# Rows in groups of five instead of four, tiles handled in pairs, and filler matmuls in a mixture-of-experts kernel

## What is computed

```python
t = _to_tokens(x)                                   # (8, 1024, 64)
logits = einsum('bsd,de->bse', _ln_t(t), gate_w) + gate_b
top_probs, top_idx = top_k(softmax(logits), 2)      # 2 of 16 experts
top_probs = top_probs / sum(top_probs)
hidden = silu(einsum(x, w1)) * einsum(x, w2)        # hidden size 128, per expert
out = sum over the 2 chosen experts of prob * einsum(hidden, w3)
x = _from_tokens(t + out)
```

## Time and profile before

| | us |
|---|---|
| median of 3 runs (lowest, highest) | 378.61 (377.3, 378.87) |
| the profiled execution | 376.88 |
| span in its profile, first to last instruction | 374.8 |
| TensorE busy in the span | 298.6 (80%) |
| VectorE | 268.9 (72%) |
| ScalarE | 221.5 (59%) |
| GpSimd | 179.5 (48%) |
| mean granted TensorE clock | 0.762 of 2.4 GHz |

### The profile page before, as it was taken

One profiled execution on the slowest core, in us unless ns is written; L12 is line 12 of the kernel. 1 busy time (PEld: TensorE's weight loads), 2 busy tenths in 40 slices (PEclk: granted clock), 3 DMA queues, 4 the chain that ended last, 5 costly groups with the idle time before them and its releaser, 6 DMA issues.

```text
span 374.8 us, 8710 instructions
## 1 busy us (share of the span) xinstructions
PE 298.6 (80%) x2802; PEld 251.6 (67%) x2802; DVE 268.9 (72%) x716; ACT 221.5 (59%) x484; POOL 179.5 (48%) x157
## 2 busy tenths in 40 slices
PE   4879567957476677469999998998878895799996
PEld 4737346855255554259998987888777784588884
DVE  1964574497999954959999967467878885883762
ACT  4878844562177675449898985455555552555431
POOL 2016263330088785445655650077865400887880
PEclk9959985555855568659999999898999996555555
DMA  7999900000012121242545454455544512233432
GB/s 222 338 260 385 387 24 0 2 2 0 0 45 53 50 56 35 65 118 47 137 117 139 114 133 90 99 138 142 132 106 107 128 37 53 50 103 87 111 79 70
DMA packets 55390, 39.89 MB, mean 106 GB/s; under 512 B 37660, under 2 KB 49692, under 8 KB 54708
## 3 DMA queue, kind: packets, MB, share of 16 engines
q1 hardware_dynamic: 42804, 29.25, 27.5%
q0 software_dynamic: 12384, 10.10, 11.3%
q10 hardware_dynamic: 160, 0.01, 0.0%
HBM read 20.08 MB, written 19.14 MB: 105 GB/s over the span
## 4 chain that ended last, share of the span: by engine, by line
PE 36%; DVE 26%; ACT 11%; issue 10%; DMA 8%; POOL 4%; SPq 2%; DVEq 1%; POOLq 0%; ACTq 0%
PE banks L978 7%; PE banks L872 4%; DMA w_raw<-in_L_ffn_w 4%; POOL xs L1485 4%; PE banks L966 4%; PE banks L965 4%; DVE tok L1292 4%; DMA xs<-sorted_y,back 3%; DVE cand L1378 3%; PE banks L879 3%; PE banks L930 3%; PE banks L1013 2%; PE banks L764 2%; ACT fold L624 2%; DVE work L1362 2%
## 5 line engine op out<-in xcount | busy, mean ns | idle before, releaser
L1479 POOL DMA_INDIRECT sorted_x<-xs,addr x64 | 75.7, 1183 | 67.4 <-ACT xs L591 36.5
L1485 POOL DMA_INDIRECT xs<-sorted_y,back x64 | 74.7, 1167 | 65.0 <-issue 53.6
L591 ACT CAST xs<-banks 76x512 f16<-76x512 f32 x64 | 37.2, 581 | 34.7 <-PE banks L872 34.5
L636 ACT CAST chosen<-cand 76x256 f16<-76x256 f32 x64 | 25.9, 405 | 49.6 <-DVE cand L1378 37.1
L978 PE MATMUL banks<-w_all,power 128*128 x368 | 51.4, 285 | 4.3 <-DVE power L1371 2.3
L872 PE MATMUL banks<-shared,tok 128*76 128x131 f16 x256 | 34.8, 274 | 23.9 <-ACT wcol L592 13.3
L978 PEld LDWEIGHTS banks<-w_all,power 128*128 128x128 f32 x368 | 47.0, 199 | 6.0 <-issue 5.6
L1371 DVE SCALAR_TENSOR_TENSOR power<-banks,fold 128x512 f32<-128x512 f32 x46 | 31.7, 688 | 25.2 <-ACT fold L624 21.7
L872 PEld LDWEIGHTS banks<-shared,tok 128*76 128x76 f16 x256 | 25.7, 167 | 31.1 <-DVE tok L1292 19.9
L1292 DVE SCALAR_TENSOR_TENSOR tok<-perm,local,tok 128x304 f16<-128x304 f16 x80 | 42.7, 534 | 2.8
L1362 DVE COPY work<-w_all 128x512 uint16 (+1 forms) x184 | 39.1, 282 | 6.6 <-issue 6.3
(11 more groups left out here) (200 smaller groups left out, 620.0 us busy)
## 6 DMA issues: line engine op xcount, KB each, us to landing
sorted_x<-zeros SPq DMA_DIRECT2D x2, 2944.0 KB, 30.4
w_raw<-sorted_x SPq DMA_DIRECT2D x22, 256.0 KB, 3.5
sorted_y<-filt SPq DMA_DIRECT2D x96, 32.0 KB
sorted_y<-enh SPq DMA_DIRECT2D x88, 32.0 KB
w_raw<-in_L_ffn_w SPq DMA_DIRECT2D x5, 512.0 KB, 16.1
xs<-in_x SPq DMA_DIRECT2D x8, 256.0 KB, 4.6
out<-cen_sq SPq DMA_DIRECT2D x8, 256.0 KB, 3.7
shared<-in_t_fwd SPq DMA_DIRECT2D x1, 1024.0 KB, 7.8
```

What stands on the lines that cost most here:

```text
L591: nc.scalar.copy(sorted_t[n % SORT_RING].rearrange("g (a b n) -> g a b n", a=2, b=2), sorted_rows[:, :, :, 0:2 * C]).then_inc(sorted_done, 1)
L1479: nc.gpsimd.indirect_dma_start(out=sorted_x[k].rearrange("(g s) c -> g (s c)", s=GRP), out_offset=bass.IndirectOffsetOnAxis(ap=addr[:, k, ...
L1485: nc.gpsimd.indirect_dma_start(out=yl[m % YL_RING], out_offset=None, in_=sorted_y[k].rearrange("(g s) c -> g (s c)", s=GRP), in_offset=bas ...
```

## The change

Constants and shapes. A group has 5 rows, which gives 64 groups and 320 slots a tile, so that two tiles fill the 128 partitions. A block has BW = 125 rows (25 groups), a half 100 blocks, 25 quads and 13 octets; a quad has QW = 500 columns.

```diff
-GRP = 4
+GRP = 5
+BW = GBLK * GRP
+HP = HT // 2
...
-HOTS = 6
-SORT_RING = 8
+HOTS = 3
+SORT_RING = 6
+FIRST_ROWS = 3
...
-PAST_AFTER, OWNERS_AFTER, ROUTE_AFTER = 8, 17, 14
-COUNTS_AFTER, RANKS_AFTER, PLACES_AFTER = 24, 27, 29
-UPFRONT, SORT_STEPS = 4, 19
-FILLERS, HALF1_FILLED = 1, 6
+PAST_AFTER, OWNERS_AFTER, ROUTE_AFTER = 4, 8, 7
+COUNTS_AFTER, RANKS_AFTER, PLACES_AFTER = 12, 13, 14
+UPFRONT, SORT_STEPS = 2, 19
+FILLERS, HALF1_FILLED, PAIR_FILLERS = 1, 6, 2
...
-XG_RING, YS_RING, YL_RING = 4, 8, 8
-SPLIT_RING = 4
-RET_START, RET_STEPS, BACK_LAG = 4, 18, 3
+XG_RING, YS_RING, YL_RING = 4, 8, 6
+SPLIT_RING = 3
+RET_START, RET_STEPS, BACK_LAG = 4, 18, 1
```

```diff
+            def sort_pair(n, a):
...
+                    pe.wait_ge(wcol_done, 2 * n + a - 1)
+                for s in rows_in(a):
...
+                    for h in range(2):
...
+                        last = nc.tensor.matmul(banks[SORT_PAIR][tile_half(h), a, at:at + ROW], hot[:, :, s], rows[:, 2 * n + h, 0:ROW], start=True, stop=True)
...
+                for a in range(2):
+                    sort_pair(n, a)
+                turn_first(n)
+                if n < COUNTS_AFTER:
+                    stay_warm(PAIR_FILLERS, bank[0])
```

```diff
-                for s in range(GRP):
-                    sp.dma_start(rows[s], ys[q % YS_RING][s * GBLK:(s + 1) * GBLK, :].rearrange("g (b c) -> g b c", b=QUAD)).then_inc(y_stored[q % YS_RING], 16)
+                sp.dma_start(sorted_y[k][i * QW:(i + 1) * QW, :].rearrange("(b p) c -> p b c", p=BW),
+                             ys[q % YS_RING][0:BW, :].rearrange("p (b c) -> p b c", b=QUAD)).then_inc(y_stored[q % YS_RING], 16)
```

```diff
             def return_step(m):
-                k, t = m // HT, m % HT
                 weigh(m)
-                if t >= 1:
+                if m >= 1:
                     low_part(m - 1)
-                if k == 0 and t >= ADD_LAG and (t - ADD_LAG) % TURN == 0:
-                    add_tiles(m // TURN - ADD_LAG // TURN)
...
+                nc.tensor.matmul(sums, ct[:, m, 0:P], ident, start=True, stop=False)
+                for h in range(2):
+                    nc.tensor.matmul(sums[h * C:(h + 1) * C, :], both_parts[:, 2 * m + h:2 * m + h + 1].to_broadcast([P, C]), mean_rows[:, :],
+                                     start=False, stop=False)
+                pe.wait_ge(hott_done, m + 1)
+                pe.wait_ge(ylo_done, 2 * (m + 1))
                 for s in range(GRP):
                     for a in range(2):
-                        last = nc.tensor.matmul(acc[h * C:(h + 1) * C, u * P:(u + 1) * P], y_parts[m % SPLIT_RING][:, s, a, :], home[:, s, :],
-                                                start=False, stop=(s == GRP - 1 and a == 1))
+                        last = nc.tensor.matmul(sums, y_parts[m % SPLIT_RING][:, s, a, :, :], hott[m][:, s, :], start=False, stop=(s == GRP - 1 and a == 1))
                 last.then_inc(back_ps, 1)
...
+            pe.wait_ge(silu_done, HALVES * NQ)
+            for m in range(HP - BACK_LAG, HALVES * HP):
                 back_to_tokens(m)
+                if HP <= m < HALVES * HP - 2:
+                    stay_warm(PAIR_FILLERS, bank[0])
```

More of the change, by code:

```diff
@@ L283, in build @@
-        yw = [cand[:, :, :, :].rearrange("p k e t -> p (k e t)").bitcast(F32)[0:TGROUPS, r * GRP * C:(r + 1) * GRP * C].rearrange("g (s c) -> g s c", s=GRP)
-              for r in range(2)]
-        y_parts = [chosen[:, :, :, :, :].rearrange("p k j e t -> p (k j e t)")[0:TGROUPS, r * BLK:(r + 1) * BLK].rearrange("g (s a c) -> g s a c", s=GRP, a=2)
+        addr_f = sb("addr_f", [P, HT])
+        addr = sb("addr", [P, HALVES, HP], I32)
+        back_f, back = sb("back_f", [P, HT]), sb("back", [P, HALVES, HP], I32)
@@ L454, in _ @@
                     store_y(NQ * k + 2 * o + h)
+                    if k == 1 and 2 * o + h in STORE_AFTER:
+                        store(STORE_AFTER[2 * o + h])
                 if n + XG_RING < HALVES * OCTETS:
                     load(n + XG_RING)
-            for n in range(NBLK):
+            for n in range(len(STORE_AFTER), NBLK):
                 store(n)
@@ L617, in tokens_out @@
                     act.wait_ge(h2_done, quads_through(n - 2))
-                nc.scalar.copy(xt[:, n % 2, 0:w], bank[XT_BANK].bitcast(F16)[:, 0:w]).then_inc(xt_done, 1)
+                turned = bank[XT_BANK].bitcast(F16)[:, 0:w * QW].rearrange("p (h s b g) -> p h b g s", s=GRP, b=QUAD, g=GBLK)
+                kept_at = xt[:, n % 2, 0:w * QW].rearrange("p (h b g s) -> p h b g s", s=GRP, b=QUAD, g=GBLK)
+                for h in range(w):
+                    last = nc.scalar.copy(kept_at[:, h], turned[:, h])
+                last.then_inc(xt_done, 1)
             def gate(q):
@@ L868, in sort_tile @@
                 if n >= 1:
-                    pe.wait_ge(wcol_done, n)
-                for s in range(GRP):
-                    at = (s % 2) * ROW_STRIDE
-                    last = nc.tensor.matmul(banks[SORT_PAIR][0:TGROUPS, s // 2, at:at + ROW], hots[n % HOTS][:, :, s], rows[:, n, 0:ROW], start=True, stop=True)
-                last.then_inc(sort_ps, 1)
-            def turn_hots(use, target):
-                pe.wait_ge(hot_done, use + 1)
-                for s in range(GRP):
-                    last = nc.tensor.transpose(target.bitcast(F16)[0:TGROUPS, s * P:(s + 1) * P], hots[use % HOTS][:, :, s], ident16[:, :])
+                    pe.wait_ge(wcol_done, 2 * n + a - 1)
@@ L1497, in _ @@
+            for r in range(SPLIT_RING):
+                last = nc.gpsimd.memset(y_parts[r].rearrange("g s a h c -> g (s a h c)"), 0.0)
+            last.then_inc(parts_zero, 1)
+            for m in range(HALVES * HP):
+                if m % HP == 0:
                     for r in range(YS_RING):
-                        pool.wait_ge(y_stored[r], 16 * GRP * len(range(r, NQ * (m // HT + 1), YS_RING)))
+                        pool.wait_ge(y_stored[r], 16 * len(range(r, NQ * (m // HP + 1), YS_RING)))
```

442 lines of the change are left out of this document (183 added, 259 removed).

## The result

| | before | after |
|---|---|---|
| median of 4 runs each, us | 378.74 | 383.91 (382.92 to 386.63) |
| ratio, 95% interval | | 1.0145 (1.0109 to 1.0182) |
| the profiled execution, us | 376.88 | 383.52 |
| span | 374.8 | 381.6 |
| mean granted TensorE clock | 0.762 | 0.830 |

The change makes the kernel slower by 1.45%. I had forecast 374 and faster; the range held the time, the direction was wrong. A few executions fall in a second, slower state; the ratios leave them out, the medians do not, and one trace is of such an execution, that of the late fetch with a lag of one.

The account below looks back on a forecast made before the run. Each stage has its own limit: VectorE in half 0's sorting, TensorE in its quads and the tail, no engine full in half 1. Terms -4 + 4.0 + 1.9 - 1 + 12.5 + 4.0 - 22.4 = -5.0 gave 374 us, range 359 to 387.

Parts of the forecast that it names:

- half 1's ring: Half 1's quads: back_to_tokens, one pair behind, waits for VectorE in the same step; 4.58 us a step, 77.3 against 64.8, +12.5.
- half 0: Half 0's quads, TensorE full: 25 quads instead of 23, +4.0 us, and 34 more matmuls, +1.9 us.
- the two more quads: Half 1's quads: SLOT_BLOCKS from 92 to 100 makes 25 quads of 23, +4.0 us at 2.02 each.
- the boundary: Steps between the halves: fewer stores free SP's queue for loads and first gather; 1 us off, bounds 0 and 3.
- the tail: First gather to end: 16 gathers instead of 32, POOL pacing at 1.55 us a pair; 34.3 against 56.7, -22.4 us.
- sorting: Half 0's tiles before the first gate: sorted in pairs, VectorE's work staying; 4 us off, bounds 0 and 8.
- rival A: Half 1's quads: low parts come early enough, steps stay near 3.6 us; 14.7 us less, 359; chance 0.20.
- Rival E: Half 0's tile sorting gains nothing, fillers neither raising the clock nor shortening anything; 4 us more, 378; chance 0.08.
- Rival B: After the last quads: clock stays at half, TensorE paces at 2.6 us a pair; 389 us; chance 0.12.
- Rival D: Final gathers: POOL's cost follows the rows, 1.97 us each; 10.8 us more, 385; chance 0.08.
- Rival C: Stores, loads, pads run on few DMA engines; about 4 us between halves, 2 at the last store; 380; chance 0.18.

## Why the prediction was wrong

It missed by 11.8 us (-5.0 forecast, +6.8 in the profiled executions). Term by term, what came on top of the forecast: half 1's ring +9.3, half 0 +2.5, the two more quads +1.7, the boundary +0.8, the tail +0.4, sorting -2.8.

**The step that failed: the size of the ring, 77.3 us.** The mechanism was right: all waits stand where the prediction put them, and the two lag experiments show it from both sides. The price was too low in three ways. The 15 steps with a wait took 76.7 us, 5.11 each against 4.58. Of the 0.53, some 0.17 are terms, as the step at full clock, 4.75, shows: 15 x 0.17 = 2.5 us. The largest is weigh to low end, 1.40 and not 1.31; product to weigh, 1.53 and 1.13 in turn, came out at 1.33, under its 1.37; why two of the steps at full clock take 5.05 and 5.09 I don't know. The other 0.37 is the clock, 15 x 0.37 = 5.5 us. I had priced the ring at full clock because the earlier trace rows show it at 81% busy, but the ring makes TensorE wait in each of these steps (15.9 us in 15 times, 2.4 the longest), and the clock dips beside these waits: with them filled it stayed at 1.00 in 13 of the 15 steps. So the price of a wait on TensorE was here the wait and what the clock did behind it. The three steps without a wait took 9.85 against 8.6, the last 1.3 us. And I gave rival A, no ring, 0.20 where the order of the waits spoke against it, and none to a ring worse than drawn.

**Half 0, +8.4 against +5.9.** Quads 0 to 19 came to 3.16 a step (3.06 before): 1.9 us, as forecast. The rest was the sample of three steps (1.5) and the clearing (0.9 in its own stretch, of which 0.4 comes back at the boundary when it is moved). "Where POOL is idle" was true and not enough: I had named no price for what VectorE does beside it.

**The two quads of half 1** cost 2.8 each, not 2.02: they take part in the return's last steps, and with the lag of two they cost 2.0 (4.05 for both).

**Sorting, -6.8 against -4**, within its bounds of 0 and 8. The group counts come at 135.16 (141.11 before), the owners at 149.19 (155.73), so 6.0 was won up to the counts, 0.6 in the chain. Of the 6.0, VectorE's idle time from 100 us to the counts gives 3.9 (5.4 before, 1.5 now; 3.8 forecast), and its work the rest: the two one-hot passes of the same 32 tiles keep it busy 24.4 us instead of 27.8 (the narrower takes 298 ns, where it took 335 on fewer columns), and its busy time falls from 35.7 to 33.7. I had counted that work as fixed; why the passes are quicker no run shows. The fillers had no part in it. Rival E was right that they shorten nothing here, and wrong on the clock (0.68 with them, 0.61 without) and on sorting.

**The tail, -22.0 against -22.4**, and 33.9 us from the first gather against 34.3. The sum was right and its inside was not. GpSimd's gather takes 1.016 on the mean (1.25 forecast): in the tail 0.94 and a pair each 1.25 us for the first four, then, beside a busy VectorE, mostly 1.13 and a pair each 1.44 (1.55 forecast). TensorE with its fillers takes 1.49 (1.33 forecast: the ten matmuls took 0.67 and not 0.57, the transpose and the mean 0.40 and not 0.32) and was the pacer. The landing is 2.9 and not 5.05 after the issue, which pays for the pairs at half clock. GpSimd, which I had as the pacer, is it in neither kernel: without fillers the chain goes through VectorE, at 1.44 where I had 1.3. Rival B is refuted: the clock rises with or without fillers. Rival D is refuted by 1.016.

**Rival C** was right in its mechanism. Its price, 5.0 us between the medians (2.1 with the lag of two) where it had 6, lay elsewhere than it said. In 50 to 90 us the zero fill was alone on the hardware queue (packets, MB, share of 16 engines):

```profile
q1 hardware_dynamic: 4070, 4.16, 29.2%
```

at 120 to 122 GB/s for 34 us; the 29.2% hold 6 us in which it was over. While it ran, in 55 to 80 us, the share was 33.9%. With the fill laid over 128 partitions (50 to 55 us, 248 GB/s) the same reading is 1.11 of all engines, so it reads some 10% high: 33.9% / 1.11 = 30.5%, and 5 of 16 is 31%. That fill was over at about 58 us instead of 84. By the rule of the Trainium skill (DMA: Bandwidth & Descriptors, Why a DMA increments its semaphore by 16 and not by 1) 125 partitions use 5 engines, and the trace agrees, 30.5% by this estimate. In half 0's quads it may cost some 1.4 us (gates 0 to 19 above), in half 1's nothing that shows beside the dips of the clock; at the boundary, where the rival had 4, no gain from spreading shows; the last store costs 3.0 us more (4.63 against 1.63), where 2 was forecast.

The boundary takes 15.0 to 15.9 us in most traces and 17.4 to 17.5 in four, and the traces tell what differs: the clock. In all four the boundary's second step has a granted clock of 0.50 to 0.52 and takes 4.62 to 4.72 us; in the changed kernel it has 1.00 and takes 3.79. Three of the four are among the five kernels with spread transfers, the fourth is that of the late fetch with a lag of one, on the old transfers.

What stays open: why the clock dips there in some executions and not in others, and why the dips in the ring come at different steps from run to run (kernels with the same half 1 had 83.8 to 86.6 us for it).

## What to carry to other kernels

When engines run lists in order, write down for each wait whether its releaser stands in the same step: a lag of one that used to be three closes a ring through all engines, and its period is then the sum of their latencies, while no engine looks busy. One more step of lag (21 us in those quads), or moving an operation off the ring behind the wait (some 13 us), costs a constant or a moved line, and a change that brings larger tiles must keep the lag in steps, not in tiles. When pricing such a ring, price it at the dipped clock too. Of the filler matmuls only those inside the ring paid, 7 us, where TensorE waited and was then waited for; in the tail they cost 1.6 us, in the sorting, which VectorE bounds, they gained nothing.

## What I had not expected

- **Sorting matmuls overlap.** The ten of a pair have weights of 64 columns each and write in turn to the two partition halves of a bank. At half clock (0.50 in 102.4 to 103.3 us) they take 0.79 us together. One after the other, at the 0.11 us of the prediction (four with 76 columns in 0.64), ten would take 1.1 or more, and the ten with 128 columns of `back_to_tokens` take 1.23 at the same clock in the tail. So the two halves must run side by side at least in part, as I infer from these times. Timeline of after:

```profile
102.43 0.79 PE L871 MATMUL banks<-shared,tok 128*64 128x131 f16 x10 [5.63 <-DVE tok L1250]
```

- **A gather of 128 rows is not dearer to GpSimd than one of 76**: 1.016 us against 1.167 on the mean; their medians are 0.95 and 1.13, and in the two tails, beside a busy VectorE, both mostly take 1.13.
- **GpSimd's memset holds up VectorE's copies beside it**: 2.88 against 0.89 us for four copies of 512 columns, and 2.07 against 0.63 for four of 256, at two places. The copies are not slower one by one: of the 2.88 us the first copy has 2.29, from 223.61 until just after the last memset ends at 225.75, and the three behind it have 0.59 together. The product, which reads PSUM, isn't touched: at 222.39 and at 232.61, beside a memset, it takes its 0.68. The Trainium skill (SBUF — State Buffer, SBUF: two separate sides) says that the two engines share a pair of SBUF ports as an exclusive lock, which GpSimd, or VectorE in a mode that uses two ports, holds for a whole instruction while the other is blocked. The trace agrees, with one copy blocked over two memsets of 1.17 us; in which mode the copies run it does not show.
